# A pre-norm decoder on one core: the order of the last token tiles at the end of two sixteen-head attentions

## The reference, cut to what matters

```
x = x + L0_attn(layernorm(x))            # 16 heads of 16, LoRA weights
x = x + L0_xattn(layernorm(x), ctx)      # latent attention with rotary tables
x = x + L0_ffn(layernorm(x))             # quantised gated feed-forward
x = x + L1_attn(layernorm(x))            # 16 heads of 16, causal, ALiBi
x = x + L1_xattn(layernorm(x), ctx, ctx) # grouped queries
x = x + L1_ffn(layernorm(x))             # eight experts, two chosen
```

```
attn = softmax(scores); out = attn @ v             # per head, 16 columns
out  = out.transpose(0, 2, 1, 3).reshape(B, L, 256)
return out @ Wo.T + bo                             # then x = x + this
```

## Time and profile before

| what | value |
|---|---|
| median of 3 runs | 834.43 us (832.11 to 836.56) |
| the profiled execution's own time | 833.54 us |
| its span, first to last instruction | 831.7 us |
| mean granted TensorE clock | 0.948 of full speed |
| PE busy | 720.5 us (87%) |
| DVE busy | 576.9 us (69%) |
| ACT busy | 430.5 us (52%) |
| POOL busy | 198.4 us (24%) |

### The profile page before, as it was taken

The page is one execution under the profiler, slowest core; times in us unless marked ns, Lnnn a source line. Parts: engine busy times, 40 slices in busy tenths (PEclk is TensorE's granted clock), DMA queues, the critical chain, the costliest instruction groups (busy, mean ns, idle before and its releaser), DMA issues. The chain is left out here.

```text
span 831.7 us, 13300 instructions
## 1 busy us (share of the span) xinstructions
PE 720.5 (87%) x4814; PEld 462.6 (56%) x4826; DVE 576.9 (69%) x1109; ACT 430.5 (52%) x896; POOL 198.4 (24%) x298
## 2 busy tenths in 40 slices
PE   5999979999998989999847469999379999759998
PEld 3555656666665656666533345566234444348886
DVE  5678568676667657676569955565578999575666
ACT  4558734544636364543649655555256767433332
POOL 2413010303123030303135314220121111351350
PEclk9999999999999999999989779999869999958999
DMA  4624422120202111110144006220010333303111
GB/s 123 184 82 138 139 67 67 47 56 21 74 10 67 29 48 29 48 42 1 26 119 86 9 12 186 64 55 2 23 36 21 83 71 83 105 2 103 51 51 51
DMA packets 49760, 52.24 MB, mean 63 GB/s; under 512 B 10116, under 2 KB 40388, under 8 KB 49588
## 3 DMA queue, kind: packets, MB, share of 16 engines
q1 hardware_dynamic: 48982, 51.03, 22.6%
q10 hardware_dynamic: 714, 0.37, 0.2%
HBM read 26.58 MB, written 2.04 MB: 34 GB/s over the span
## 5 line engine op out<-in xcount | busy, mean ns | idle before, releaser
L427 DVE TENSOR_REDUCE a_nm<-ps 128x2 f32<-128x512 f32 (+1 forms) x112 | 75.4, 688 | 28.2 <-PE ps L723 18.1
L2480 DVE TENSOR_REDUCE x_nm<-ps 128x2 f32<-128x512 f32 x128 | 85.0, 687 | 13.0 <-PE ps L2621 10.8
L2565 ACT ACTIVATE x_pt<-ps 128x1024 f32<-128x1024 f32 x64 | 62.5, 1021 | 33.9 <-PE ps L2649 33.2
L1389 ACT ACTIVATE m_junk<-ps,m_nm 128x256 bf16<-128x256 f32 x128 | 58.7, 486 | 30.3 <-DVE m_nm L1233 30.3
L1518 PE MATMUL ps<-m_xp,m_mp 128*128 128x512 f32 x288 | 73.4, 395 | 1.0 <-DVE m_wr L1221 1.0
L1185 POOL TENSOR_SCALAR fw<-fw,finv 128x256 f32<-128x256 f32 x24 | 11.6, 485 | 232.8 <-PE ps L1596 232.8
L2621 PE MATMUL ps<-kx,a_qs 96*128 96x256 bf16 x256 | 52.3, 291 | 8.5 <-DMA a_qs<-a_ks 6.5
L1518 PEld LDWEIGHTS ps<-m_xp,m_mp 128*128 128x128 f32 x288 | 51.3, 188 | 13.1 <-issue 3.2
L3049 PE MATMUL ps<-x_xp,x_wp 128*128 128x512 f32 x216 | 55.1, 406 | 0.0
L1201 DVE TENSOR_TENSOR m_qcs<-ps,mw_tab 64x512 f32<-64x512 f32 x64 | 44.1, 689 | 7.6 <-PE ps L1518 4.3
L3049 PEld LDWEIGHTS ps<-x_xp,x_wp 128*128 128x128 f32 x216 | 41.2, 196 | 8.5
(11 more groups left out here) (305 smaller groups left out, 1692.2 us busy)
## 6 DMA issues: line engine op xcount, KB each, us to landing
a_qs<-a_parts SPq DMA_DIRECT2D x48, 128.0 KB
a_ks<-a_parts SPq DMA_DIRECT2D x48, 128.0 KB
m_q<-m_qs SPq DMA_DIRECT2D x32, 128.0 KB
x_gb<-scr_g SPq DMA_DIRECT2D x8, 512.0 KB, 3.7
fw<-in_f_w SPq DMA_DIRECT2D x12, 256.0 KB
a_qs<-a_ks SPq DMA_DIRECT2D x48, 64.0 KB
mw_wq<-in_m_wq SPq DMA_DIRECT2D x8, 256.0 KB, 2.9
mw_wo<-in_m_wo SPq DMA_DIRECT2D x8, 256.0 KB, 2.8
```

Of the source, the lines that this page charges most:

```text
L427: dve.tensor_reduce(dst, src, AX.X, ALU.max, negate=True).then_inc(mx_done.sem, 1)
L1389: act.activation(junk[:, n % 4, :], c.ps[:, S_BANKS[k % 4], qt * SEQ:(qt + 1) * SEQ], ACT.Exp, bias=nm[:, k // 4, one], accum_out=den[:, k ...
L2480: dve.tensor_reduce(nm[:, n % ITEMS, QT * u:QT * u + QT], c.ps[:, u % 2, :].rearrange("p (t k) -> p t k", t=QT), AX.X, ALU.max, negate=Tru ...
L2565: act.activation(pt[:, n % 2, kt, :], c.ps[:, 2 + 2 * kt:4 + 2 * kt, :].rearrange("p b n -> p (b n)"), ACT.Exp, scale=SCALE).then_inc(exp_ ...
```

## The change

In both attentions PE issues turn_outputs(6) and turn_outputs(7) in front of output_project(5), and DVE issues quotients(6) and quotients(7) in front of residual(5). The last tile, whose banks are its own, no longer waits for a bank of tile 6: turn_outputs(7) does not wait for `on_done` of tile 6, turn_quotients(7) not for `onT_done` of tile 6, and output_project(7) not for `x_done` of tile 6. No instruction is added or removed, and none changes its shape; three waits of PE are left out.

```diff
--- before.py
+++ after.py
@@ -504,9 +504,9 @@
                 quotients(5)
                 outputs(N - 1)
                 residual(4)
-                residual(5)
                 quotients(6)
                 quotients(7)
+                residual(5)
                 if scales is not None:
                     scales.vector(dve)
                 residual(6)
@@ -796,7 +796,7 @@
                     pe.wait_ge(out_done.sem, out_done.at((6, 8, 14, 16)[t // QT]))
                     if t == 0:
                         pe.wait_ge(mx_done.sem, mx_done.at(UNITS * N))
-                    else:
+                    elif t < TT - 1:
                         pe.wait_ge(on_done.sem, on_done.at(t))
                     for g in range(GROUPS):
                         mm = pe.transpose(c.ps[:, banks_of(t)[0], g * P:(g + 1) * P],
@@ -805,7 +805,7 @@
 
                 def turn_quotients(t):
                     pe.wait_ge(on_done.sem, on_done.at(t + 1))
-                    if t:
+                    if 0 < t < TT - 1:
                         pe.wait_ge(onT_done.sem, onT_done.at(t))
                     for dt in range(DT):
                         mm = pe.transpose(c.ps[:, banks_of(t)[1], dt * P:(dt + 1) * P],
@@ -912,9 +912,9 @@
                 product(N - 1, 1)
                 output_project(4)
                 turn_quotients(5)
-                output_project(5)
                 turn_outputs(6)
                 turn_outputs(7)
+                output_project(5)
                 if scales is not None:
                     scales.tensor(pe)
                 turn_quotients(6)
```

## The result

| | before | changed |
|---|---|---|
| median of 6 runs each | 833.73 us (831.12 to 836.56) | 827.63 us (826.82 to 829.79) |
| ratio to before | | 0.9938, 95% interval 0.9911 to 0.9964 |
| the profiled execution: time, span | 833.54, 831.7 us | 827.96, 826.2 us |
| turn_quotients(5) to the end of the last residual, first attention | 8.43 us | 5.43 us |
| the same, second attention | 8.37 us | 5.26 us |

The kernel became faster by 6.1 us by the medians; a median of 828.4 had been forecast. The ratio is an estimate of its own and not that of the two medians: it stands for 5.2 us, with an interval of 3.0 to 7.4.

What follows compares the result with a forecast made beforehand. Both attention ends were taken as bound by a chain going round PE, DVE and ACT, not by busy PE. Savings of 2.9 and 3.1 us, -6.0 from the median 834.43, gave 828.4; range 825.0 to 831.8.

Steps and rivals of the forecast that it cites:

- Steps 1 to 3: First attention's end: transposes of tiles 6 and 7 over by 105.98, projection 5 from 105.82, residual(5) 107.01 to 107.43.
- Step 4: First attention's end: scale product, turn_quotients(6) until about 107.25, ACT's copy until 107.66; DVE's scale reductions cost nothing.
- Steps 5 and 6: First attention's end: projection 6 starts at 107.75, projection 7 follows without waiting, residual(7) ends at 110.21, 2.9 us less.
- The sum: Ends of both attentions: 2.9 us less in the first, 3.1 in the second, -6.0 together, bounds -5.2 to -6.2.
- The rival of the half-speed stretch: Behind the shifted ends: one more stretch of TensorE at half speed costs 3.2 us, giving 831.6; chance 0.13.
- Only the removed wait pays: Both ends: projection 6 starts as late as before, only projection 7's removed wait counts, 1.7 us, giving 832.7; chance 0.08.
- Slower: Start of the latent stage, 111 to 125, at half speed: costs up to 11.5 us, giving 839.9; chance 0.03.

Runs made afterwards that it cites:

- that of the second: A second set of 6 runs of the unaltered changed kernel against the kernel before; 827.44 us beside 834.25, ratio 0.9919.
- the waits alone: The kernel before, in its old order, with the last tile's three waits left out; 831.82 us, ratio 0.9985; again 831.88 us, 0.9969.
- the order alone: The changed kernel with the three waits of the last tile put back; 830.51 us, ratio to before 0.9969.
- DVE's order put back: The changed kernel with residual(5) again in front of quotients(6) and (7) on DVE; 831.53 us.

## Why the prediction was right

The time, 827.63, lies 0.8 from the forecast of 828.4, and in the range. Of the 0.8, 0.7 are the median of before, which the forecast took as 834.43 from three executions and which is 833.73 with three more. By its own steps:

- **Steps 1 to 3 held, to 0.01 but for the last.** Worked out from turn_quotients(5)'s start: projection 5 at 1.10 (measured 1.09), quotients(6) at 0.85 (0.85), residual(5) at 2.29. This last came at 2.16: the quotients of tiles 6 and 7 and the residual follow each other every 0.64 and 0.67 us, less than the 0.72 that a tile was given.
- **Step 4**: turn_quotients(6) started at 2.09, behind the scale product, as laid out, and ACT's copy at 2.55 (2.56 worked out). The scale sums on DVE ran behind residual(5) under the cover named, and cost nothing.
- **Steps 5 and 6**: projection 6 at 2.98 (worked out 3.03), residual(7)'s end at 5.43 (5.49). In the second attention 5.26 (5.32). What released projection 6 in both was ACT's copy; for the second attention the prediction had named residual(5), which there was over 0.23 before projection 6 started, at 584.51. Since copy and residual lay close together, the wrong link cost only 0.05. Projections 6 and 7 came in one stream, with 0.79 and 0.86 between the residuals (0.87 worked out). Projection 7's wait put back singly is worth 0.92 and 0.86, the 0.84 of the prediction.
- **The sum** was -6.0; the ends gave -6.11, the medians -6.1. That the two medians differ by just the ends is partly luck: the stretches repeat to 0.01 us, but the scatter moves either median by a microsecond or more, and the ratio of the first set stands for 5.2 us, that of the second for 6.8.
- **The rival of the half-speed stretch** was real in kind and mis-sized in its term: I priced one more by 620 to 628 at 3.2 us. Falls in the latent stage are cheaper (four of them 2.4 us together), but up to six come in one execution where before and changed had two, and one stretch of the feed-forward costs 2.3 more when it is long; together they reach 4.7. The changed kernel itself had four more falls and the long stretch in its second profile, and neither in its first. The latent stage, whose start I had seen at 1.00, is where most of the falls that differ stand.
- **Only the removed wait pays** is refuted by the kernel with the waits alone (3.61, not 1.7) and by the order alone.
- **Slower**: the start of the latent stage, 111 to 125, was granted 1.00. In four of the experiments' profiles a fall did come between 116 and 126, in three for some 3.4 us, with DVE's order put back for 6.8: a fall can come in that place, but none took the over 7 of 14 us that the rival needed. The new end has ten transposes in a row and was granted 1.00 from 104 to 111. The Trainium skill ("TensorE: Matmul & The Clock Gate", Part 4, PE-mode transpose) says that transposes do not count as PE activity the way other matmuls do; nothing here shows a loss by it.

## What to carry to other kernels

At the end of a stage, where tiles go round several engines, write down each link's start from the timeline and move the work that is ready in front of the work that waits, on every engine that has it in its queue: on one engine alone (PE here, with DVE's order kept) it gained nothing beyond the waits. A resource of its own for the last tile pays in full only if each wait for the old one is taken out (0.24, 0.92 and 1.11 us here), and such a wait costs not only its own length but all that is queued behind it. Where the time scatters by as much as the change is worth, judge the change by the stretch it acts on, and the time by rounds enough to average the clock, or by executions with like clocks.

## What was not expected of the hardware

The granted clock fell inside a stage in which PE was busy for 192.77 of 208 us, with no idle time of PE over 1 us close in front of the fall at 146 (0.97 and 0.53 are the gaps on the timeline of 140 to 150). The falls last some 3.4 us (one of 6.8 with DVE's order put back). In the first profile of the waits alone and the second of the changed kernel they come 36 to 38 us apart up to 262; in others they stand at 121, 182 and 295, or at 122, 221 and 296. Whether they come differs between executions of one program. How often they come differs between programs: a mean clock of 0.936 to 0.943 in 20 of 20 executions of the waits alone, in 12 of 35 of the kernel before. What decides it stays open. It is not alone the time at which the stage starts, counted from the span's start: the first product came at 111.9 us both with the waits alone (first profile, four falls up to 320) and with the order alone (two, at 219 and 294). No run here shifted the stage alone by known steps often enough to show it.
